# Stacked keys and queries written to neighbouring partitions in 4 KB runs

## The chip, the cores and the metric

The kernel runs on 1 core of one Trainium2 chip. The metric is the device time of one execution in microseconds (us). A change of about 1% is what a measurement of this kernel can tell from none.

## The reference

A gated cross-attention block and a feed-forward block, float32, over 64 sequences of 128 tokens with 256 features; 16 heads of 16. The causal mask is inside the attention, and the result of each block is added through a tanh gate:

```python
def _L0_xattn_ref(q, k, v, Wq, Wk, Wv, Wo, bo):
    qh = jnp.einsum('bse,hed->bhsd', q, Wq)
    kh = jnp.einsum('bse,hed->bhsd', k, Wk)
    vh = jnp.einsum('bse,hed->bhsd', v, Wv)
    scores = jnp.einsum('bhsd,bhtd->bhst', qh, kh) / jnp.sqrt(d)
    scores = jnp.where(causal, scores, -1000000000.0)
    att = jax.nn.softmax(scores, axis=-1)
    out = jnp.einsum('bhst,bhtd->bhsd', att, vh)
    return concat(out) @ Wo.T + bo

def _L0_ffn_ref(x, ...):                       # _tlin(x, w, s) = einsum('bsi,oi->bso', x, w) * s
    h = silu(_tlin(x, w1_w, w1_s)) * _tlin(x, w2_w, w2_s)      # 256 -> 1024
    h = gelu(_tlin(h, h1_w, h1_s))                             # 1024 -> 1024
    h = gelu(_tlin(h, h2_w, h2_s))                             # 1024 -> 1024
    return _tlin(h, w3_w, w3_s)                                # 1024 -> 256

x = x + tanh(g_xattn) * _L0_xattn_ref(_layernorm(x), ctx, ctx, ...)
x = x + tanh(g_ffn) * _L0_ffn_ref(_layernorm(x), ...)
```

## The kernel before

Two sequences ("rows", `ROWS = 2`) make a block, and there are 32 blocks. While the feed-forward of block n - 1 runs, the attention of block n is computed, and its projections for block n + 1 are begun. All engines walk through one list written by hand, `ORDER` (`PROLOGUE` for the first block): each engine picks out the steps that are its own and runs them in that order. A "+" behind a step means that it works for the next block. The waits between the engines are semaphores.

The steps that matter here are these. `Q` and `K` project queries and keys on TensorE (PE). ScalarE writes their high part in a rounded float32, and VectorE the rest, the low part, to `q_parts` and `k_parts`, which hold [128 features, part, row, half of the features, 128 tokens]. To score at nearly full float32 precision, a head needs high and low parts of queries against high and low parts of keys, four products, and the kernel stacks them in the contraction dimension: `q4` and `k4` hold each feature four times, on different partitions (`COPIES = 4`), queries as high, low, high, low and keys as high, high, low, low. `k4` has, besides, an index e for the two halves of the features; entries of the other half are zero and stay so, from a memset at the start. In this way one matmul of 128 by 256 computes two heads.

[...]

- `write_parts` (steps `qw` and `kw`) waits until the parts are ready and until the copies of the block before have landed, and writes 512 KB to `q_saved` or `k_saved` (L338).
- `place_parts` (steps `kr.0`, `qr.0`, `qr.1`, `kr.1`: keys or queries of row 0 or 1) waits for this write and for the scores that still read the old copies, and issues the transfers back: for keys, 8 a row of 64 KB (L356), for queries, 4 a row of 128 KB (L351), all in runs of 1 KB. Copy number c fills the partitions c, c + 4, c + 8 and so on.
- In `scores` (steps `S.0` to `S.7`, L939), PE waits, at the first step of each row (S.0 and S.4), for all copies of queries and keys of that row; 16 counts a transfer.

In ORDER the issues of SP come as `D.6 ... D.7 kr.0+ qr.0+ qr.1+ lr+` at the end of one walk and `kr.1 lc+ lx+ D.0 lt+` at the start of the next. `D.t` is the transpose of the probabilities of step t by DMA (L366), and waits for POOL's parts of them and for PE's products with the values (`PV`, L955); `lr` loads the residual xres (L324), `lc`, `lx` and `lt` load the inputs of the next block. PE meets S.0 just ahead of the last feed-forward layer (`L4`) of the same walk, and S.4 between the third and the fourth output tile of the first one (`L1`). `rx` is POOL's addition to xres (L453).

Of the kernel before, what the change touches and what calls it, by code (L numbers as in the profile page):

```python
# [11 lines left out]
F32 = mybir.dt.float32  # L12
F32R = mybir.dt.float32r
# [5 lines left out]
P = 128  # L19
ROWS = 2  # L20
# [39 lines left out]
def program(nc, x, xT_in, cT_in, gains, attn_w, bo, w_all, scale_cols, w3s, out):  # L60
# [5 lines left out]
    KE = E // P  # L66
    KF = F // P
    NQ = ROWS * H // 4
    QROW = H // 4
# [16 lines left out]
    HALF = P // 2  # L86
# [3 lines left out]
    with ExitStack() as ctx:  # L90
        def sb(name, shape, dt=F32):
            return ctx.enter_context(nc.sbuf_tensor(name, shape, dt))
# [4 lines left out]
        def sem(name):  # L97
            return ctx.enter_context(nc.semaphore(name))
# [32 lines left out]
        COPIES = 4  # L131
        q_parts = sb("q_parts", [P, 2, ROWS, KE, P], F32R)
        k_parts = sb("k_parts", [P, 2, ROWS, KE, P], F32R)
        q4 = sb("q4", [P, ROWS, QROW, KE, P], F32R)
        k4 = sb("k4", [P, ROWS, QROW, 2, KE, P], F32R)
        q_saved = nc.dram_tensor("q_saved", [P, 2, ROWS, KE * P], F32, kind="Internal").ap()
        k_saved = nc.dram_tensor("k_saved", [P, 2, ROWS, KE * P], F32, kind="Internal").ap()
        vs = sb("vs", [P, ROWS, H, VCOLS], BF16)
        v_rest = sb("v_rest", [P, ROWS, E])
        PSLOTS = 4  # L140
# [68 lines left out]
        q_placed = [sem("q_placed0"), sem("q_placed1")]  # L209
        k_placed = [sem("k_placed0"), sem("k_placed1")]  # L210
# [35 lines left out]
        def wait(eng, s, value):  # L246

            if not isinstance(value, int) or value > 0:
                eng.wait_ge(s, value)
# [55 lines left out]
        def _(sp):  # L305
            def hold(s, value):
                if not isinstance(value, int) or value > 0:
                    sp.wait_ge(s, value)
                    sp.sem_inc(sp_waited)  # L309
# [21 lines left out]
            def write_parts(n, kind):  # L331

                parts, saved = (q_parts, q_saved) if kind == "qw" else (k_parts, k_saved)
                hold(*((q_hi_ready, KE * n + KE) if kind == "qw" else (k_hi_ready, n + 1)))
                hold(*((q_lo_ready, KE * n + KE) if kind == "qw" else (k_lo_ready, n + 1)))
                for placed in q_placed if kind == "qw" else k_placed:
                    hold(placed, 16 * COPIES * (1 if kind == "qw" else 2) * n)
                sp.dma_start(saved.rearrange("p a r x -> p (a r x)"),  # L338
                             parts[:].rearrange("p a r m t -> p (a r m t)").bitcast(F32))\
                    .then_inc(q_written if kind == "qw" else k_written, 16)  # L340

            def place_parts(n, kind, row):

                if kind == "kr" and isinstance(n, int) and n == 0 and row == 0:
                    sp.wait_ge(keys_cleared, 1)
                hold(q_written if kind == "qr" else k_written, 16 * n + 16)
                for ready in scores_ready:
                    hold(ready, NQ // 2 * n + QROW // 2 * (row - 1))
                for copy in range(COPIES):
                    if kind == "qr":  # L350
                        sp.dma_start(q4[copy:P:COPIES, row].rearrange("p j m t -> p j (m t)").bitcast(F32),  # L351
                                     q_saved[:, copy % 2, row].rearrange("(p j) x -> p j x", j=QROW))\
                            .then_inc(q_placed[row], 16)
                    else:
                        for e in range(2):
                            sp.dma_start(k4[e * HALF + copy:(e + 1) * HALF:COPIES, row, :, e]  # L356
                                         .rearrange("p j m t -> p j (m t)").bitcast(F32),
                                         k_saved[e * HALF:(e + 1) * HALF, copy // 2, row]
                                         .rearrange("(p j) x -> p j x", j=QROW)).then_inc(k_placed[row], 16)

            def transpose_probs(n, t):

# [17 lines left out]
            def body(n, ffn_on=True, attn=True, next_head=True, weights=False):  # L380
                for kind, k, ahead in table(n):
                    blk = n + ahead
                    here = next_head if ahead else attn
                    if kind == "lx" and here and not (isinstance(blk, int) and blk == 0):
                        load_x(blk)
                    if kind == "lt" and here and not (isinstance(blk, int) and blk == 0):
                        load_xT(blk)
                    if kind == "lr" and here:
                        load_residual(blk)
                    if kind == "lc" and here and not (isinstance(blk, int) and blk == 0):  # L390
                        load_c(blk)
                    if kind in ("qw", "kw") and here:
                        write_parts(blk, kind)
                    if kind in ("qr", "kr") and here:
                        place_parts(blk, kind, k)
                    if kind == "D" and here:
                        transpose_probs(blk, k)
                    if kind == "mv" and ffn_on:
                        move_x1(n - 1)
                    if kind == "sy" and not (isinstance(n, int) and n < 2):  # L400
                        store(n - 2)
# [8 lines left out]
            with sp.If(sp.value_load(flag[0:1, 0:1]) > 0):  # L410
                sp.wait_ge(chunk_rounded, CHUNKS)
                sp.wait_ge(chunk_tested, CHUNKS)
                for i in range(CHUNKS, 2 * CHUNKS):
                    slot, use = i % STAGES, i // STAGES
                    at = i % CHUNKS * CHUNK
# [484 lines left out]
        def _(pe):  # L900
# [30 lines left out]
            def scores(n, t):  # L931

                row, j = t // QROW, t % QROW
                wait(pe, masked_ready, n * NQ + t - 1)
                if j == 0:
                    wait(pe, q_placed[row], 16 * COPIES * (n + 1))
                    wait(pe, k_placed[row], 16 * COPIES * 2 * (n + 1))
                for m in range(KE):
                    last = pe.matmul(s_bank[t % SBANKS][:, m * TOK:(m + 1) * TOK].rearrange("p (e t) -> p e t", e=2),  # L939
                                     q4[:, row, j, m], k4[:, row, j, :, m], start=True, stop=True)  # L940
                last.then_inc(scores_ready[t % SBANKS], 1)

            def probs_values(n, t):
# [15 lines left out]
            def run(general, first):  # L959
# [17 lines left out]
                def body(n, ffn_on=True, attn=True, next_head=True, weights=False):  # L977
# [8 lines left out]
                    for kind, k, ahead in table(n):  # L986
# [38 lines left out]
                        if kind == "S" and here:  # L1025
                            scores(blk, k)
# [89 lines left out]
```

## Time and profile before

| | |
|---|---|
| Median of 3 runs | 1858.6 us (1854.09 to 1867.01) |
| The profiled execution | 1868.9 us, its span 1867.1 us |
| Busy share: PE, VectorE, ScalarE, GpSimd | 93%, 74%, 71%, 58% |
| Mean granted TensorE clock | 0.975 |
| Transfers of keys a block | 16 of 64 KB |
| Transfers of queries a block | 8 of 128 KB |
| Write of each to DRAM a block | 1 of 512 KB |

How to read it: one execution was recorded by the hardware profiler. Times are us from the start of the span. PE is TensorE's matmuls, PEld its weight loads, DVE VectorE, ACT ScalarE, POOL GpSimd, SP SyncE, and "SPq" SyncE's queue of instructions, which holds the DMA issues. L939 is line 939 of the kernel. A block is 54.8 us from 200 us on. The "chain" is followed back from the last instruction, at each step to what released it.

### The profile page before, as it was taken

How to read it: one execution, taken by the hardware profiler on the slowest of the kernel's cores; microseconds unless marked ns; L12 is line 12 of the kernel's file. 1: busy time of each engine (PE TensorE's matmuls, PEld its weight loads, DVE VectorE, ACT ScalarE, POOL GpSimd, SP SyncE). 2: the span in 40 equal slices, each digit the busy share in tenths (PEclk: the TensorE clock that was granted, in tenths of full speed). 3: DMA queues.
4: the chain of work that ended last, by engine and by line, in shares of the span. 5: the costliest groups of instructions: out<-in, count | busy, mean ns of one | idle time of the engine just before them, and what ended most of it. 6: DMA issues, size and time to landing. Idle time of an engine off the chain costs nothing.

```text
span 1867.1 us, 39954 instructions
## 1 busy us (share of the span) xinstructions
PE 1730.6 (93%) x11014; PEld 1482.3 (79%) x11014; DVE 1389.0 (74%) x3059; ACT 1319.2 (71%) x3014; POOL 1075.4 (58%) x1389
## 2 busy tenths in 40 slices
PE   3279999999999999999999999999999999999998
PEld 2268888888888888888888888888888888888876
DVE  4477777788777777877777877777777777787774
ACT  3356777777677877777777767777767777776764
POOL 2365556655555666555665655566555566565552
PEclk7579999999999999999999999999999999999999
DMA  8944544445444444454444545444445444454420
GB/s 281 152 125 114 142 114 115 125 118 139 125 125 120 119 113 135 124 140 115 117 124 115 140 118 138 116 115 125 118 124 140 115 119 125 112 140 118 125 53 16
DMA packets 399643, 231.39 MB, mean 124 GB/s; under 512 B 287232, under 2 KB 377600, under 8 KB 398080
## 3 DMA queue, kind: packets, MB, share of 16 engines
q1 hardware_dynamic: 397456, 219.25, 45.6%
q10 hardware_dynamic: 2160, 11.81, 2.2%
q8 instruction: 13, 0.21, 0.1%
q14 instruction: 14, 0.11, 0.0%
HBM read 113.53 MB, written 41.94 MB: 83 GB/s over the span
## 4 chain that ended last, share of the span: by engine, by line
PE 56%; SPq 29%; issue 6%; DMA 6%; DVE 1%; POOL 1%; ACT 0%; POOLq 0%; DVEq 0%
PE ffn L964 45%; SPq L356 15%; SPq L351 8%; PE work L904 6%; SPq L366 4%; DMA k<-k_saved 4%; DMA pT<-p_parts 2%; PE s_bank L939 2%; PE pv L955 2%; SPq L324 1%; SPq L309 0%; PE work L1044 0%; DMA aw<-in_attn_w 0%; DVE full L639 0%; DVE full L632 0%
## 5 line engine op out<-in xcount | busy, mean ns | idle before, releaser
L964 PE MATMUL ffn<-hb,W 128*128 128x512 f32 x2048 | 510.5, 399 | 1.2 <-POOL hb L501 1.2
L964 PE MATMUL ffn<-ha,W 128*128 128x512 f32 x2048 | 477.9, 393 | 1.3 <-POOL ha L496 1.3
L964 PEld LDWEIGHTS ffn<-ha,W 128*128 128x128 f32 x2048 | 382.0, 188 | 84.4 <-POOL ha L496 2.7
L646 DVE TENSOR_REDUCE full<-ffn 128x256 f32<-128x512 f32 x512 | 346.2, 686 | 136.7 <-PE ffn L964 107.3
L964 PEld LDWEIGHTS ffn<-hb,W 128*128 128x128 f32 x2048 | 375.6, 188 | 77.0 <-POOL hb L501 2.1
L809 ACT ACTIVATE probs<-probs,exp_bias 128x128 f32<-128x128 f32 x1024 | 323.8, 391 | 81.9 <-DVE exp_bias L614 80.7
L464 POOL TENSOR_TENSOR p_parts<-probs,p_parts 128x512 f16<-128x512 f32 x256 | 301.6, 1178 | 20.4
L462 POOL CAST p_parts<-probs 128x512 f16<-128x512 f32 x256 | 157.2, 614 | 207.4 <-ACT probs L809 165.0
L604 DVE SCALAR_TENSOR_TENSOR probs<-s_bank,rstd,causal 128x512 f32<-128x512 f32 x256 | 191.4, 748 | 97.4 <-PE s_bank L939 96.9
L964 PE MATMUL ffn<-x2T_hi,W 128*128 128x256 f32 x1024 | 253.3, 286 | 0.7 <-DVE x2T_lo L742 0.5
L827 ACT ACTIVATE full<-full,cols 128x256 f32<-128x256 f32 x512 | 253.4, 495 | 0.0
L964 PE MATMUL ffn<-x2T_lo,W 128*128 128x256 f32 x1024 | 251.4, 283 | 0.0
L501 POOL TENSOR_TENSOR hb<-full,hb 128x256 fp32r<-128x256 f32 x256 | 189.2, 739 | 84.1 <-ACT full L827 75.3
L496 POOL TENSOR_TENSOR ha<-full,ha 128x256 fp32r<-128x256 f32 x256 | 185.8, 740 | 38.0 <-ACT ha L841 34.1
L826 ACT ACTIVATE ha<-full,cols 128x256 fp32r<-128x256 f32 x256 | 129.3, 505 | 107.0 <-DVE full L646 106.6
L964 PEld LDWEIGHTS ffn<-x2T_hi,W 128*128 128x128 f32 x1024 | 195.9, 191 | 2.7 <-DVE y L714 0.8
L964 PEld LDWEIGHTS ffn<-x2T_lo,W 128*128 128x128 f32 x1024 | 196.0, 191 | 0.0
L612 DVE TENSOR_REDUCE negmax<-probs 128x4 f32<-128x512 f32 x256 | 173.8, 679 | 2.2
L939 PE MATMUL s_bank<-k,q 128*128 128x256 f32 x512 | 113.9, 315 | 64.5 <-DMA k<-k_saved 39.7
L850 ACT ACTIVATE full<-ffn,half_s 128x256 f32<-128x256 f32 x256 | 119.5, 467 | 47.0 <-PE ffn L964 46.0
L964 PE MATMUL ffn<-W,ha 128*128 128x256 f32 x1024 | 146.7, 288 | 6.1 <-DVE full L646 6.0
L826 ACT ACTIVATE hb<-full,cols 128x256 fp32r<-128x256 f32 x256 | 128.2, 501 | 31.7 <-DVE full L646 30.7
(81 smaller groups left out, 2413.2 us busy)
## 6 DMA issues: line engine op xcount, KB each, us to landing
k<-k_saved SPq DMA_DIRECT2D x512, 64.0 KB, 2.3
q<-q_saved SPq DMA_DIRECT2D x256, 128.0 KB, 2.7
k_saved<-k_parts SPq DMA_DIRECT2D x32, 512.0 KB, 2.7
q_saved<-q_parts SPq DMA_DIRECT2D x32, 512.0 KB, 2.7
wnat<-in_ffn_w ACTq DMA_DIRECT2D x11, 1024.0 KB, 11.7
xT<-in_x_T SPq DMA_DIRECT2D x32, 256.0 KB, 3.2
cT<-in_ctx_T SPq DMA_DIRECT2D x32, 256.0 KB, 2.7
x_in<-in_x SPq DMA_DIRECT2D x32, 256.0 KB, 2.9
```

Of the source, the lines that this page charges most:

```text
L356: sp.dma_start(k4[e * HALF + copy:(e + 1) * HALF:COPIES, row, :, e] .rearrange("p j m t -> p j (m t)").bitcast(F32), k_saved[e * HALF:(e + ...
L462: pool.tensor_copy(p_parts[:, t % 2, 0], probs[:, t % PSLOTS]).then_inc(p_hi_ready, 1)
L464: pool.tensor_tensor(p_parts[:, t % 2, 1], probs[:, t % PSLOTS], p_parts[:, t % 2, 0], ALU.subtract)\
L496: pool.tensor_tensor(ha_lo[:, k], full[:, k % 4], ha_hi[:, k], ALU.subtract)\
L501: pool.tensor_tensor(hb_lo[:, k], full[:, k % 4], hb_hi[:, k], ALU.subtract)\
L604: dve.scalar_tensor_tensor(probs[:, slot], s_bank[t % SBANKS][:].rearrange("p (h t) -> p h t", h=4), rstd[:, t // QROW:t // QROW + 1], cau ...
L612: dve.tensor_reduce(negmax[:, slot], probs[:, slot], AX_X, ALU.max, negate=True).then_inc(max_ready, 1)
L646: dve.tensor_reduce(full[:, m % 4], src[:].rearrange("p (a t) -> p t a", a=2), AX_X, ALU.add).then_inc(done, 1)
L809: last = act.activation(probs[:, slot, h], probs[:, slot, h], ACT.Exp, bias=exp_bias[:, slot, h:h + 1])
L826: act.activation(hi[:, m], f, ACT.Gelu, scale=scales[:, m:m + 1]).then_inc(hi_sem, 1)
L827: act.activation(f, f, ACT.Gelu, scale=scales[:, m:m + 1]).then_inc(hi_sem, 1)
L964: return pe.matmul(dst, w, h, **flags)
```

## The change

Three edits. The tensors in DRAM are laid out [part, row, feature, ...] and not [feature, part, row, ...]. The four copies of a feature no longer lie on four neighbouring partitions: each half of 64 partitions has its groups of 16 partitions by copy, and partition d of a group holds the four features 4d to 4d + 3 in its four slots j, which lie one behind the other in DRAM (4 KB). So one transfer fills 32 neighbouring partitions, for queries with the high and then the low part, for keys with the same part twice (a repeat with a step of zero in the source). And in `k4` the index e stands ahead of j, so that the 4 KB are in one piece there too. Keys take 4 transfers of 128 KB a row and not 8 of 64 KB; queries stay at 4 of 128 KB. The number in the wait for the keys follows. ORDER is the same.

```diff
-        k4 = sb("k4", [P, ROWS, QROW, 2, KE, P], F32R)
-        q_saved = nc.dram_tensor("q_saved", [P, 2, ROWS, KE * P], F32, kind="Internal").ap()
-        k_saved = nc.dram_tensor("k_saved", [P, 2, ROWS, KE * P], F32, kind="Internal").ap()
+        k4 = sb("k4", [P, ROWS, 2, QROW, KE, P], F32R)
+        q_saved = nc.dram_tensor("q_saved", [2, ROWS, P, KE * P], F32, kind="Internal").ap()
+        k_saved = nc.dram_tensor("k_saved", [2, ROWS, P, KE * P], F32, kind="Internal").ap()
...
                 for placed in q_placed if kind == "qw" else k_placed:
-                    hold(placed, 16 * COPIES * (1 if kind == "qw" else 2) * n)
-                sp.dma_start(saved.rearrange("p a r x -> p (a r x)"),
-                             parts[:].rearrange("p a r m t -> p (a r m t)").bitcast(F32))\
+                    hold(placed, 16 * COPIES * n)
+                sp.dma_start(saved.rearrange("a r p x -> p (a r) x"),
+                             parts[:].rearrange("p a r m t -> p (a r) (m t)").bitcast(F32))\
                     .then_inc(q_written if kind == "qw" else k_written, 16)
...
-                for copy in range(COPIES):
-                    if kind == "qr":
-                        sp.dma_start(q4[copy:P:COPIES, row].rearrange("p j m t -> p j (m t)").bitcast(F32),
-                                     q_saved[:, copy % 2, row].rearrange("(p j) x -> p j x", j=QROW))\
-                            .then_inc(q_placed[row], 16)
-                    else:
-                        for e in range(2):
-                            sp.dma_start(k4[e * HALF + copy:(e + 1) * HALF:COPIES, row, :, e]
-                                         .rearrange("p j m t -> p j (m t)").bitcast(F32),
-                                         k_saved[e * HALF:(e + 1) * HALF, copy // 2, row]
-                                         .rearrange("(p j) x -> p j x", j=QROW)).then_inc(k_placed[row], 16)
+                for e in range(2):
+                    for copy in range(2):
+                        at = e * HALF + copy * HALF // 2
+                        if kind == "qr":
+                            src = q_saved[:, row, e * HALF:(e + 1) * HALF].rearrange("a (d j) x -> a d (j x)", j=QROW)
+                            sp.dma_start(q4[at:at + HALF // 2, row].rearrange("p j m t -> p (j m t)").bitcast(F32), src)\
+                                .then_inc(q_placed[row], 16)
+                        else:
+                            src = k_saved[copy, row, e * HALF:(e + 1) * HALF].rearrange("(d j) x -> d (j x)", j=QROW)
+                            sp.dma_start(k4[at:at + HALF // 2, row, e].rearrange("p j m t -> p (j m t)").bitcast(F32),
+                                         src.unsqueeze(0).broadcast_to([2, HALF // QROW, QROW * KE * P]))\
+                                .then_inc(k_placed[row], 16)
...
-                    wait(pe, k_placed[row], 16 * COPIES * 2 * (n + 1))
+                    wait(pe, k_placed[row], 16 * COPIES * (n + 1))
...
-                                     q4[:, row, j, m], k4[:, row, j, :, m], start=True, stop=True)
+                                     q4[:, row, j, m], k4[:, row, :, j, m], start=True, stop=True)
```

## Rows read from the trace of the kernel before

**Rows 1.** The page: span, TensorE, the chain's shares, and POOL's longest group.

```profile
span 1867.1 us, 39954 instructions
...
PE 1730.6 (93%) x11014; PEld 1482.3 (79%) x11014; DVE 1389.0 (74%) x3059; ACT 1319.2 (71%) x3014; POOL 1075.4 (58%) x1389
...
PE 56%; SPq 29%; issue 6%; DMA 6%; DVE 1%; POOL 1%; ACT 0%; POOLq 0%; DVEq 0%
...
L464 POOL TENSOR_TENSOR p_parts<-probs,p_parts 128x512 f16<-128x512 f32 x256 | 301.6, 1178 | 20.4
```

**Rows 2.** The chain that ended last, one block: start us, us, what.

```profile
978.38 1.23 SPq L366
...
996.52 2.18 DMA k<-k_saved
...
998.75 0.51 PE s_bank L939 x2
```

**Rows 3.** PE's timeline: start us, us, instructions, idle before in brackets.

```profile
990.13 0.50 PE L939 MATMUL s_bank<-k,q 128*128 128x256 f32 x2 [0.20 <-DMA q<-q_saved]
...
998.75 0.51 PE L939 MATMUL s_bank<-k,q 128*128 128x256 f32 x2 [1.23 <-DMA k<-k_saved]
```

**Rows 4.** Waits of PE, 1200 to 1748.4 us: us in total, times, longest.

```profile
PE s_bank L939 <- DMA k<-k_saved: 13.3, 10, 1.9
PE s_bank L939 <- DMA q<-q_saved: 2.3, 10, 0.4
```

**Rows 5.** Stretches: us, busy us by engine, granted clock, DMA share, GB/s.

```profile
974.40:1029.20 54.80, 53.19 (x346) 45.78 (x345) 42.34 (x96) 40.72 (x95) 33.16 (x44) 1.00 0.47 124
...
976.00:977.00 1.00, 1.00 (x21) 0.90 (x20) 0.00 (x0) 0.88 (x4) 0.92 (x2) 1.00 1.06 417
...
992.00:999.00 7.00, 5.77 (x49) 5.55 (x48) 6.70 (x16) 5.96 (x16) 4.71 (x6) 1.00 0.47 136
...
20.00:30.00 10.00, 0.44 (x2) 0.44 (x3) 5.48 (x3) 1.91 (x1) 0.00 (x0) 0.67 0.89 274
...
110.50:115.60 5.10, 5.10 (x24) 5.10 (x25) 3.59 (x7) 3.44 (x11) 3.02 (x3) 0.50 0.32 103
115.80:121.70 5.90, 5.30 (x45) 5.13 (x44) 4.22 (x10) 3.79 (x9) 5.07 (x7) 1.00 1.05 211
```

**Rows 6.** Timeline of SyncE's queue over the same block: start us, us, issues.

```profile
974.40 0.41 SPq L378 DMA_DIRECT2D out<-y  x1
975.29 0.33 SPq L338 DMA_DIRECT2D q_saved<-q_parts  x1
976.80 2.80 SPq L366 DMA_TRANSPOSE pT<-p_parts  x2
980.05 5.02 SPq L356 DMA_DIRECT2D k<-k_saved  x8
985.42 5.19 SPq L351 DMA_DIRECT2D q<-q_saved  x8
990.78 0.46 SPq L324 DMA_DIRECT2D xres<-in_x  x1
992.09 5.03 SPq L356 DMA_DIRECT2D k<-k_saved  x8
```

**Rows 7.** The page's DMA issues: KB each, median us from issue to landing.

```profile
k<-k_saved SPq DMA_DIRECT2D x512, 64.0 KB, 2.3
q<-q_saved SPq DMA_DIRECT2D x256, 128.0 KB, 2.7
k_saved<-k_parts SPq DMA_DIRECT2D x32, 512.0 KB, 2.7
q_saved<-q_parts SPq DMA_DIRECT2D x32, 512.0 KB, 2.7
```

**Rows 8.** Waits of the whole span, POOL's for the residual.

```profile
POOL xres L453 <- DMA xres<-in_x: 97.1, 30, 4.5
```

**Rows 9.** Block 0: timelines of SyncE's queue and of PE.

```profile
19.06 5.13 SPq L356 DMA_DIRECT2D k<-k_saved  x8
...
29.56 1.22 PE L939 MATMUL s_bank<-k,q 128*128 128x256 f32 x4 [10.93 <-DMA q<-q_saved]
...
43.29 0.89 PE L939 MATMUL s_bank<-k,q 128*128 128x256 f32 x2
```

## The prediction, made before the changed kernel ran

> **What bounds the kernel now.** I read the page first, then the chain of work that ended last over one steady block, then the timelines of TensorE and of SyncE's queue over the same block, then the waits, the landings of the transfers and, last, stretches for the load of the DMA engines. The page [rows 1] gives PE 93% of the span, and the chain 56% PE and 29% SyncE's queue. So PE is the bound and is nearly full, but the thread that fixes its pace runs through the queue that issues the transfers. The chain [rows 2] shows the loop: PE ends a product with the values, the queue issues the transpose of the last probabilities at 978.38, and only then, in program order, the copies of keys and queries; the last copy of keys lands 2.18 us after its issue and frees the matmul of S.4 at 998.75. The PE timeline [rows 3] shows the price on PE: 0.20 us idle before S.0 (waiting for queries) and 1.23 us before S.4 (waiting for keys of row 1). Over ten blocks the waits [rows 4] are 13.3 us for keys and 2.3 us for queries, so 1.56 us a block. That is all that an earlier arrival can return; PE's other work fills the rest of a block of 54.80 us [rows 5].
>
> The queue's timeline [rows 6] has its work from 980.05 on: 8 keys issues (5.02 us), 8 queries issues (5.19 us, both rows), xres, 8 keys issues (5.03 us). One issue is (5.02 - 0.04) / 8, some 0.63 us with its gap. The DMA engines are busy for 0.47 of a block on average [rows 5]: they are no bound as long as each transfer is spread over all 16.
>
> **The change part by part.**
>
> *Fewer issues.* Eight of 16 keys issues go: 8 x 0.63 = 5.0 us of SyncE's queue a block, 2.5 us of it ahead of the queries and 2.5 us in the last group. If all else is equal, this takes the 1.56 us of waits away. Queries stay at eight issues. Bytes stay: 512 KB of keys a row and block, in 4 transfers of 128 KB instead of 8 of 64 KB, and 4 x 128 KB of queries.
>
> *The spread over engines, the step that decides.* Read the shapes and not the sizes. Before, each copy has 16 partitions (keys) or 32 partitions (queries) as its outer count on both sides: 16 engines can each be given an equal part. After, the destination is 32 neighbouring partitions, but the source is (2, 16, 1024): for queries the 2 are the high and the low parts, 256 KB apart, and for keys the 2 are a repeat with step zero. Neither folds with the 16 behind it. If the split is made along the outer count, a transfer has two parts, and so two engines, each with 16 runs of 4 KB. Should it always be the same two, they carry every byte of the keys and queries, one transfer behind the other. No transfer of the trace before has so small an outer count (the ones touched lead with 16, 32 or 128), so no row shows this; I take it as the likeliest for its shape alone: whatever deals out the parts by the outer count can't make 16 of 2.
>
> The Trainium skill speaks against this change in the same direction (DMA: Bandwidth & Descriptors, section Why a DMA increments its semaphore by 16 and not by 1, and the row "Use all 16 engines" of its Rules for kernel authors): the engine count is the largest up to 16 that divides the slowest count of both sides, the lowest-numbered engines are used, and a leading zero-stride broadcast of c copies confines a DMA to c engines. By that rule k is 2 here, always the same pair; no row of before shows a case of it.
>
> *Price of a confined transfer.* The nearest rows for long runs are of 976 to 977 us, where the store of the output and the 512 KB write of q_saved, in 4 KB runs, stand back to back on the same queue: 417 GB/s at a share of 1.06 [rows 5]. That is 417 / 16 = 26.1 GB/s for one engine, with no gap between two transfers. 128 KB is 131,072 bytes; half of it is 65,536 bytes, / 26.1 = 2.51 us. The other end is the rate with 1 KB runs: 992 to 999 us moved 136 GB/s at a share of 0.47, so 136 / 0.47 / 16 = 18.1 GB/s, which makes 3.62 us. The runs are 4 KB, so I take 2.51. A block has 16 such transfers: 40.2 us on two engines.
>
> *What is late, and by how much.* From the first keys issue (980.05) to S.4 (998.75) are 18.7 us now. After: 0.6 us for the first issue; about 0.3 us of the transposes still under way (0 to 1); 16 x 2.51 = 40.2; xres, which stands among them (256 KB over 16 engines at 18.1 GB/s is 0.9); and 2.1 us of latency, the 2.3 us to landing of a 64 KB copy [rows 7] less the 0.23 us that its 4 KB an engine takes. Sum 44.1 us, so S.4 starts 25.4 us later. Half way, S.0 needs the first eight: 0.6 + 0.3 + 20.1 + 2.1 = 23.1, at 1003.2 instead of 990.13, 13.0 us later; this is inside the 25.4 and not on top of it. PE is in order: behind S.0 stand the last layer (L4), X2, S.1 to S.3 and the first L1 steps, 998.75 - 1.23 - 990.13 = 7.4 us, which fit between the two waits. Behind S.4 stands everything to the next keys issue, 54.8 - 18.7 = 36.1 us that shift with PE. POOL waits for xres (97.1 us in 30 times now [rows 8]); it lands near 1014. Behind it are four POOL operations; even at 1178 ns each, that of the split [rows 1], they end before 1020, so S.4 stays the last. cT, x_in and the first transposes queue up behind the keys; some 3 us of engine time that K and PV don't need before 5 to 7 us after S.4.
>
> *The clock.* In the first block PE sat idle for 10.93 us ahead of S.0 [rows 9]; in 20 to 30 us the granted clock is 0.67 (a fall from 2.4 to 1.2 GHz on the way), and 0.50 in 110.5 to 115.6, where 24 matmuls take 5.10 us; at full clock 45 take 5.30 us [rows 5], so 24 take 2.8. Two idle stretches of that kind in every block would take the clock down each time. After S.0 the 7.4 us at half speed are under 15 us and still end at about 1018, ahead of 1024; after S.4 up to 5.10 - 2.8 = 2.3 us are lost. I take 1.5 (0 to 2.3).
>
> *Small parts.* The write of q_saved and k_saved now goes out in 1 KB runs: 32 KB an engine at 18.1 instead of 26.1 GB/s, 1.8 instead of 1.25 us. Its landing (2.7 us, [rows 7]) has cover: issued at 975.29, read from 982 on at the earliest. Without cover it would be 0.55 us. The matmul reads the keys in two runs of 128 with another step, 282 ns or so before and after: nothing. The wait counts change by number only. SyncE's 5.0 us are gained and hidden behind the landing.
>
> *Sum.* 25.4 + 1.5 = 26.9 us a block. Copies for blocks 1 to 31 are made in steady order: 31 x 26.9 = 834. Block 0 has its copies in the prologue: first keys issue 19.06, S.4 at 43.29 [rows 9]; with 44.1 us it is at 63.2, 20 us later, and the weight loads share the engines (274 GB/s at 0.89 in 20 to 30 us); I take 25 (0 to 50). The profiled execution took 1868.9 us with a span of 1867.1: 1868.9 + 834 + 25 = 2728. It is 10.3 us above the median of the three runs, 1858.6, so the prediction is 2718, say **2720**.
>
> A check of the order: the two engines would be busy for 40.2 us, plus the rest of the block's traffic. Of 0.47 x 54.8 = 25.8 us, the keys and queries are now 2 MB / 16 / 18.1 GB/s = 7.2; 18.6 remain. 58.8 us is over the 54.8 of a block, so even with all waits hidden it could not be as fast as before: at least 4 x 31 = 124 us more, 1983.
>
> **The rivals.**
>
> *All 16 engines, as the text of the change has it.* Something splits the 32 partitions and not the 2, or the pair moves on from transfer to transfer. The last of queries row 0 is then issued 2.5 us earlier, S.0 waits for nothing; the last of keys row 1 is issued at about 992.0 and with 2.7 us lands at 994.7, ahead of 997.5 where PE gets there. It gains 1.56 x 31 = 48 us: 1810. For it: it is all that is needed, and a 128 KB copy of queries lands in 2.7 us now [rows 7]. Against it: the leading 2 of the source. It decides where S.4's wait is gone. It would be faster, the other side. Chance 0.11.
>
> *Only the keys confined* (the step of zero treated apart, queries on 16). The engine time up to S.4 is 8 x 2.51 + 8 x 0.45 + 0.9 = 24.6, with 3.0 around it 27.6: 8.9 us a block later, 276 in all, 2135. Against it: the two sources have the same counts. Chance 0.04.
>
> *Spread over 16, and nothing gained:* S.4 then waits for something else, such as slower writes into 32 neighbouring partitions; at 3 us more landing the 1.56 us would be gone. 1859. Chance 0.03.
>
> **How the numbers follow.** Confined to one pair has 0.82, and 2720 is its time. Its bounds: without clock loss and prologue 1859 + 31 x 25.4 = 2646; with some of the wait absorbed, or a rate a little above, down to 2450; with the 18.1 GB/s the transfers take 57.9 us and the time is 2720 + 31 x 17.7 = 3269, which I count only in part, as the runs are 4 KB: 3100. The range 2450 to 3100 leaves out the other three cases (0.18) and little of this one. About 1% is what a measurement of this kernel can tell from no change. Faster by over 1% is the first rival, 0.11; within 1% the third, 0.03; slower 0.82 + 0.04 = 0.86.
>
> **What the profile after would show.** To landing of a keys or queries copy 4.6 us where nothing is queued, and over 10 us in the median, as they queue up; PE idle about 13 us before S.0 and 6 to 13 us before S.4 (less when the clock is low between them), named by keys and queries; a block of about 82 us; PE under 70% busy; granted clock under 1.0 in every block; the mean share of the DMA engines lower, not higher; the keys issues 256. Wrong it is if the copies land in under 4 us and the block is near 53 us, which is the first rival; if queries land in 3 us and only keys late, it is the second.

## The result, and the profile after

The changed kernel takes 2755.2 us in the median of 4 runs (2750.0 to 2757.7), the kernel before on the same chips 1861.2 us. The ratio is 1.480, its 95% interval 1.474 to 1.486. The prediction was 2720 us, and the mechanism put first in it is the one that the profile shows.

The spans of the two profiled executions differ by 881 us (the medians by 894). Where they come from can be read from the first keys issue of each block. Before, that of block 1 is at 97.6 us and that of block 31 at 1750.9: 55.1 us a block. After, they are at 116.0 and 2604.9: 83.0 us a block. So 18.3 us are lost in block 0, 30 x 27.9 = 836 in the steady blocks, and 26.9 in block 31 and what follows it; together 881.

The page of the changed kernel, against [rows 1] and [rows 7]: span, busy shares, granted clock, the chain, and the issues of keys and queries.

```profile
span 2748.1 us, 39669 instructions
...
PE 1838.9 (67%) x11014; PEld 1594.0 (58%) x11014; DVE 1398.3 (51%) x3059; ACT 1316.8 (48%) x3014; POOL 1071.8 (39%) x1389
...
PEclk6587888988888988888888788878888887898889
...
PE 40%; SPq 34%; DMA 21%; issue 4%; DVE 1%; POOL 0%; ACT 0%; POOLq 0%; DVEq 0%
...
k<-k_saved SPq DMA_DIRECT2D x256, 128.0 KB
q<-q_saved SPq DMA_DIRECT2D x256, 128.0 KB
k_saved<-k_parts SPq DMA_DIRECT2D x32, 512.0 KB, 3.0
```

PE is busy for 108 us more, since part of its work runs at a lower clock, but it fills only two thirds of the span, and DMA's share of the chain has gone from 6% to 21%. For keys and queries the page has no time to landing any more; in the two experiments below that confine only one kind, the column is empty for that kind alone.

PE's timeline in one steady block, against [rows 3]: start us, us, idle before in brackets. The first is S.0, the second S.4.

```profile
1382.84 0.80 PE L940 MATMUL s_bank<-k,q 128*128 128x256 f32 x2 [13.77 <-DMA q<-q_saved]
...
1404.29 0.77 PE L940 MATMUL s_bank<-k,q 128*128 128x256 f32 x2 [12.36 <-DMA k<-k_saved]
```

Where PE waited for 0.20 and 1.23 us, it waits for 13.8 and 12.4.

SyncE's queue in the same block, against [rows 6]:

```profile
1359.20 2.72 SPq L358 DMA_DIRECT2D k<-k_saved  x4
1362.18 14.09 SPq L354 DMA_DIRECT2D q<-q_saved  x8
1376.46 2.15 SPq L324 DMA_DIRECT2D xres<-in_x  x1
1379.32 10.44 SPq L358 DMA_DIRECT2D k<-k_saved  x4
...
1441.69 2.60 SPq L358 DMA_DIRECT2D k<-k_saved  x4
```

The first four issues are as quick as those before (0.65 us each). Then the queue blocks: 8 queries issues take 14.09 us and not 5.19. The chain of the same block shows the step from free to blocked (start us, us, what): the third queries issue takes 0.92 us, and the fourth 2.29, which is about the time that one transfer needs. It has the landing of the last keys transfer too: 16.73 us after its issue, where it was 2.18 [rows 2].

```profile
1363.47 0.92 SPq L354
...
1364.42 2.29 SPq L354
...
1387.42 16.73 DMA k<-k_saved
```

Stretches of the same block, against [rows 5] (granted clock, DMA share and GB/s are the last three columns):

```profile
1359.20:1441.70 82.50, 56.19 (x346) 48.80 (x345) 42.55 (x97) 40.67 (x94) 33.08 (x44) 0.86 0.36 83
1364.00:1366.00 2.00, 2.00 (x12) 1.66 (x11) 1.53 (x4) 1.12 (x3) 0.10 (x1) 1.00 0.13 53
1366.00:1368.00 2.00, 1.82 (x9) 1.25 (x8) 1.61 (x4) 0.90 (x3) 1.15 (x1) 1.00 0.13 53
1370.00:1374.00 4.00, 0.00 (x0) 0.00 (x0) 0.00 (x0) 0.00 (x0) 0.00 (x0) 0.87 0.13 51
```

This is the line to look for. While the queue is full of keys and queries, the mean busy share of the 16 DMA engines is 0.13, that is 2 of 16 (0.125), and they move 51 to 53 GB/s, 26 a busy engine. The profile has no row for each engine, but this is what fourteen engines standing still and two at work would give. Several transfers were waiting all that time; were they on different pairs, the share would be higher, so it is one pair for all. In the kernel before, the share was 0.47 with the keys of row 1 on the queue [rows 5].

### The profile page after: what moved, and what is told of

Read it like the earlier page. It is cut to its first block, busy times and chain, and to the rows that moved or that the text cites. A ratio compares the mean times of both kernels' runs of the same rounds, so it can differ in the third digit from the quotient of the medians.

```text
span 2748.1 us, 39669 instructions
## 1 busy us (share of the span) xinstructions
PE 1838.9 (67%) x11014; PEld 1594.0 (58%) x11014; DVE 1398.3 (51%) x3059; ACT 1316.8 (48%) x3014; POOL 1071.8 (39%) x1389
## 4 chain that ended last, share of the span: by engine, by line
PE 40%; SPq 34%; DMA 21%; issue 4%; DVE 1%; POOL 0%; ACT 0%; POOLq 0%; DVEq 0%
PE ffn L965 33%; DMA k<-k_saved 19%; SPq L354 16%; SPq L358 12%; PE work L905 4%; SPq L367 3%; SPq L324 2%; PE s_bank L940 2%; PE pv L956 1%; DMA cT<-in_ctx_T 1%; DMA pT<-p_parts 1%; SPq L309 0%; PE work L1045 0%; DMA aw<-in_attn_w 0%; POOL p_parts L465 0%
## 5 line engine op out<-in xcount | busy, mean ns | idle before, releaser
L940 PE MATMUL s_bank<-k,q 128*128 128x256 f32 x512 | 130.6, 352 | 834.1 <-DMA q<-q_saved 452.9
L940 PEld LDWEIGHTS s_bank<-k,q 128*128 128x128 f32 x512 | 94.4, 223 | 851.5 <-DMA q<-q_saved 427.3
L454 POOL TENSOR_TENSOR xres<-xres,bo_tg 128x512 f32<-128x512 f32 x32 | 42.5, 1327 | 728.4 <-DMA xres<-in_x 728.4
L633 DVE SCALAR_TENSOR_TENSOR full<-full,ffn 128x256 f32<-128x256 f32 x256 | 107.2, 419 | 430.5 <-ACT full L851 423.9
L878 ACT ACTIVATE x2T_hi<-work 128x256 fp32r<-128x256 f32 x64 | 24.6, 384 | 576.6 <-PE work L1045 576.6
L965 PE MATMUL ffn<-x2T_hi,W 128*128 128x256 f32 x1024 | 298.2, 320 | 0.5 <-DVE x2T_lo L743 0.5
L965 PE MATMUL ffn<-x2T_lo,W 128*128 128x256 f32 x1024 | 293.9, 315 | 0.0
L965 PEld LDWEIGHTS ffn<-x2T_hi,W 128*128 128x128 f32 x1024 | 234.9, 229 | 1.6 <-DVE x2T_lo L743 0.7
L965 PEld LDWEIGHTS ffn<-x2T_lo,W 128*128 128x128 f32 x1024 | 232.8, 227 | 0.0
```

Source lines behind the costliest of these rows:

```text
L965: return pe.matmul(dst, w, h, **flags)
```

## The experiments

Each was timed beside the kernel before, on the same chip.

**Exchange the two outer dimensions.** Nothing else changes: the same bytes, run length, number of transfers and set of 32 partitions; on them the two parts now lie interleaved.

```diff
-src = q_saved[:, row, e * HALF:(e + 1) * HALF].rearrange("a (d j) x -> a d (j x)", j=QROW)
+src = q_saved[:, row, e * HALF:(e + 1) * HALF].rearrange("a (d j) x -> d a (j x)", j=QROW)
...
-             src.unsqueeze(0).broadcast_to([2, HALF // QROW, QROW * KE * P])
+             src.unsqueeze(1).broadcast_to([HALF // QROW, 2, QROW * KE * P])
```

> The changed kernel with the two outer dimensions of each source exchanged (16 feature groups outside, the 2 inside); the two parts lie interleaved on the 32 partitions. Bytes, runs of 4 KB, number of transfers (4 a row for keys and for queries), partitions as a set and the writes to DRAM stay. Theory 'outer count sets the number of engines': transfers are back on 16 engines, waits of PE for keys and queries vanish, near 1810 us (1795 to 1830), block near 53.3 us, issues of 0.6 us. Rival 'neighbouring partitions': writing into 32 neighbours is what is slow, it stays near 2755. Rival 'a repeated source is slow': keys stay slow, queries recover, near 2110.

Measured: 1813.1 us, ratio 0.974 (0.968 to 0.980). The page and SyncE's queue of this kernel:

```profile
k<-k_saved SPq DMA_DIRECT2D x256, 128.0 KB, 2.8
q<-q_saved SPq DMA_DIRECT2D x256, 128.0 KB, 2.7
...
PE 83%; DVE 8%; issue 4%; DMA 2%; POOL 1%; ACT 1%; DVEq 0%; SPq 0%; POOLq 0%; ACTq 0%
```

```profile
1211.58 2.50 SPq L358 DMA_DIRECT2D k<-k_saved  x4
1214.34 5.14 SPq L354 DMA_DIRECT2D q<-q_saved  x8
1220.84 0.41 SPq L324 DMA_DIRECT2D xres<-in_x  x1
1221.96 2.46 SPq L358 DMA_DIRECT2D k<-k_saved  x4
...
1265.58 2.50 SPq L358 DMA_DIRECT2D k<-k_saved  x4
```

PE's waits of this kernel over ten blocks, 1200 to 1740 us, against [rows 4]:

```profile
PE ffn L965 <- DVE x2T_lo L743: 2.9, 10, 0.4
PE ffn L965 <- DVE full L647: 1.8, 10, 0.2
PE ffn L965 <- DVE y L715: 1.3, 6, 0.3
```

The whole loss is gone, and both waits for keys and queries with it; the queue's share of the chain falls from 29% before to 0%. The block is 54.0 us. Rivals that blame the neighbouring partitions or the repeat in the source fall: both are still there. Timed again beside other runs it was the same:

> e1_outer16 unchanged, to see its gain once more beside the others, probably on another chip: ratio to the kernel before 0.974 again, near 1813 us.

Measured: 1812.0 us, ratio 0.974 (0.969 to 0.980).

**The same partitions, transfers cut in their halves.** To be sure that the interleaving doesn't matter, each transfer of the changed kernel is issued as two of 16 partitions, which leaves every byte where the change puts it (counts in the waits doubled).

```diff
+for a in range(2):
+    src = q_saved[a, row, e * HALF:(e + 1) * HALF].rearrange("(d j) x -> d (j x)", j=QROW)
+    sp.dma_start(q4[at + a * 16:at + a * 16 + 16, row]..., src)     # keys likewise
```

> The changed kernel with exactly the same bytes on the same partitions, but each transfer of 32 partitions cut in its two halves of 16 (outer count 16 on both sides, 64 KB): 16 transfers of keys and 16 of queries a block. Outer count theory: all on 16 engines, the loss is gone. By the 0.44 us issues seen for such transfers in e2_queries_outer2 the last keys issue of a block ends some 15.7 us after the first, landing at 17.8 against 18.7 before: 1820 to 1840. Rival 'the arrangement on neighbouring partitions is slow': stays far above 1861. Rival 'the number of issues sets the time': with 32 issues in place of 24, slower than before, 1900.

Measured: 1843.3 us in the median of ten runs from 1828.8 to 1853.4, ratio 0.992 (0.989 to 0.994), 3 us over the expected stretch. Its queue:

```profile
1223.93 3.57 SPq L360 DMA_DIRECT2D k<-k_saved  x8
1227.76 7.36 SPq L355 DMA_DIRECT2D q<-q_saved  x16
...
1236.54 3.55 SPq L360 DMA_DIRECT2D k<-k_saved  x8
```

The loss is gone here too, so the place on the partitions costs nothing. 32 issues are a little faster than 24 before (0.8%, which is less than the 1% that one measurement tells from none): a transfer to 16 neighbouring partitions takes 3.57 / 8 = 0.45 us to issue, one with two outer dimensions some 0.63. What goes with the time is not the count of issues, but when the last one is out: 16.2 us after the first keys issue here, 17.1 before, and 12.8 in the first experiment.

**Only one kind confined.** First queries with the 2 outside and keys in halves of 16 partitions, then the other way round. The edits to the changed kernel, the first for keys, the second for queries:

```diff
-sp.dma_start(k4[at:at + HALF // 2, row, e]..., src.unsqueeze(0).broadcast_to([2, HALF // QROW, QROW * KE * P]))
+for a in range(2):
+    sp.dma_start(k4[at + a * 16:at + a * 16 + 16, row, e]..., src)
```

```diff
-sp.dma_start(q4[at:at + HALF // 2, row]..., src)
+for a in range(2):
+    src = q_saved[a, row, e * HALF:(e + 1) * HALF].rearrange("(d j) x -> d (j x)", j=QROW)
+    sp.dma_start(q4[at + a * 16:at + a * 16 + 16, row]..., src)
```

> The changed kernel with keys in 8 transfers a row of 16 partitions each (outer count 16 on both sides, no repeat in the source, 4 KB runs); queries stay with the 2 outside. Outer count theory: 8 transfers a block are confined to one pair of engines, and queue there: S.4 comes 0.6 + 4.8 + 8 x 2.51 + 0.9 + 1.3 + 2.1 = 29.8 us after the first keys issue and not 18.7, so 11 us a block, 1861 + 31 x 11 = 2200, up to 2270 with the clock's fall. Rival 'a repeated source is slow': near 1861. Rival 'neighbouring partitions': queries are still 32 neighbours, keys 16 neighbours, near 2755.

Measured: 2344.0 us, ratio 1.259 (1.250 to 1.269).

> The changed kernel with queries in 8 transfers a row of 16 partitions each (outer count 16 on both sides, 4 KB runs); keys stay with the repeat of 2 outside. Outer count theory: S.4 comes 26.6 us after the first keys issue and not 18.7, so 8 us a block, 1861 + 31 x 8 = 2109, up to 2170 with the clock's fall and the prologue. Were each kind on a pair of engines of its own, this and e2_queries_outer2 would each keep about half of the loss of the change or more, 2300 or above; with one pair for both, the two losses together are less than the whole, since part of each wait is hidden. Rival 'a repeated source is slow': nearly all the loss stays, near 2700.

Measured: 2283.0 us, ratio 1.227 (1.217 to 1.236).

Each kind is confined by itself, with the repeat in the source and without it; so the step of zero is not the point. But both are 75 to 175 us above what was expected of them, 2 to 6 us a block, and their sum, 483 + 422 = 905 us over the kernel before, is not less than the whole loss (894). The time is in the transfers: in the second kernel S.4 comes 30.4 us after the first keys issue, and not 26.6. The first keys issue, S.4 and stretches of that kernel:

```profile
1264.64 2.60 SPq L359 DMA_DIRECT2D k<-k_saved  x4
...
1295.00 0.58 PE L941 MATMUL s_bank<-k,q 128*128 128x256 f32 x2 [2.05 <-DMA k<-k_saved]
```

```profile
1271.00:1273.00 2.00, 2.00 (x10) 1.45 (x8) 1.76 (x3) 0.99 (x3) 0.73 (x1) 1.00 0.56 166
1275.00:1277.00 2.00, 0.00 (x0) 0.00 (x0) 0.00 (x0) 0.00 (x0) 0.22 (x1) 1.00 0.56 161
1286.00:1292.00 6.00, 6.00 (x43) 5.97 (x42) 4.94 (x11) 4.14 (x10) 1.63 (x3) 0.80 0.13 52
```

While spread transfers run beside the confined ones, a busy engine moves 166 / 0.56 / 16 = 18.5 GB/s, and when the pair is alone, 52 / 0.13 / 16 = 25. My estimate used 26 throughout. The 18.5 is a mean over all busy engines and does not show the pair's own rate. That the pair too was slower is an estimate: from 1267 to 1294 us the share in stretches of 1 us is never under 0.12, so the pair was never idle, and up to S.4 each of its engines has 8 x 64 KB of keys, 16 x 4 KB of queries and 16 KB of xres to move, 606,000 bytes in 27 to 28 us, some 22 GB/s. That covers the sign and about the size of the miss; what the engines contend for (the DRAM side, or the gaps between short shares) no run here tells apart.

The sum of the two losses was to be less than the whole with one pair for both. In the mean of blocks 5 to 29 of the traces it is, as far as the transfers go: S.4 comes 31.9 and 30.7 us after the first keys issue instead of 18.8, which is 13.1 + 11.9 = 25.0 us later against 26.0 in the changed kernel (44.8 us). But behind S.4 each of the three kernels loses 1.4 to 2.0 us a block besides (38.2, 37.6 and 38.0 us instead of 36.2 to the next keys issue), and so the sum has this loss twice. That keys and queries did not have a pair each is shown by the changed kernel itself: its share stays at 0.13 from 1364 us on, when both kinds were waiting.

**Length of the runs against the number of issues.** The first experiment with keys in 8 transfers a row again, so 24 issues a block as before, but runs of 4 KB on 16 engines:

```diff
+for a in range(2):
+    sp.dma_start(k4[at + a:at + HALF // 2:2, row, e]..., src)
```

> e1_outer16 with keys in 8 transfers a row of 64 KB (16 partitions at a step of 2, outer count 16, 4 KB runs), so as many issues as before. It tells the number of issues from the length of the runs. Theory 'the wait is for the queue's issues': as before, within 1% of 1861, PE waits 1.2 to 1.6 us at S.4 for keys. Rival 'run length': long runs land so much earlier that it is as fast as e1_outer16.

Measured: 1852.2 us in the median of nine runs, ratio 0.994 (0.990 to 0.998). PE's waits over ten blocks, 1200 to 1740 us, of the profiled execution, which was the slowest of the nine (1867.2 us):

```profile
PE s_bank L940 <- DMA k<-k_saved: 11.7, 10, 1.4
...
PE s_bank L940 <- DMA q<-q_saved: 0.6, 3, 0.3
```

Of the 1.56 us of waits a block [rows 4], 1.2 are still there. Runs of 4 KB bring 0.3 us a block at most (9 us in all, less than the 1% that one measurement tells from none), the eight issues fewer the rest. That is the part of the change which was sound.

**The clock's part.** PE idles twice a block in the changed kernel, and the clock falls. To take this alone, matmuls that nobody reads were put in ahead of the two waits, in time that PE has to spare there.

```diff
+if j == 0 and not (isinstance(n, int) and n == 0):
+    for i in range(40):                        # second try: 60 if row == 0 else 53
+        pe.matmul(s_bank[t % SBANKS][:], W[:, 0:P], W[:, 0:BANK], start=True, stop=True)
```

> The changed kernel as it is, as the base for e6_filled on the same chip: near 2755 us.

Measured: 2761.5 us, ratio 1.485 (1.480 to 1.490).

> The changed kernel with 40 matmuls of 512 columns put in ahead of PE's wait at S.0 and at S.4 (their results are overwritten); at full clock they take some 8.6 us, less than the 13.8 and 12.4 us for which PE waits there anyway. It measures the clock's part alone. Theory 'the fall of the clock costs 1.3 to 1.5 us a block, after S.4': the granted clock goes from 0.83 to near 0.95 or more, and 31 x 1.4 = 43 us come back, near 2712. Rival 'the block's end is set by the transfers, the clock costs nothing': within 1% of e7_change_again with 10 us or less gained.

Measured: 2752.3 us, ratio 1.479 (1.473 to 1.486), only 9 us less. This run doesn't decide: up to 4.6 and 3.3 us of idle time were left ahead of S.0 and S.4, and the clock was still at half right behind S.4. PE's timeline there shows matmuls at 0.41 us:

```profile
1411.11 0.77 PE L943 MATMUL s_bank<-k,q 128*128 128x256 f32 x2 [3.25 <-DMA k<-k_saved]
1411.67 0.41 PE L968 MATMUL ffn<-x2T_hi,W 128*128 128x256 f32 x1
```

So the idle time had to be filled further:

> e6_filled left 4.6 us of PE idle ahead of S.0 and 3.3 us ahead of S.4, and the clock was still at half behind S.4 (matmuls of the next layer at 410 ns). Here 60 matmuls stand ahead of S.0 (13 us at full clock) and 53 ahead of S.4 (11.5 us), so that less than 1 us of either wait is left idle. Theory 'the clock's fall costs 1.3 to 2.8 us a block after S.4': the matmuls behind S.4 run at 280 ns, from S.4 to the next keys issue it is 36.1 us again as before the change, and the time is 40 to 85 us under the changed kernel on the same chip. Rival 'the clock costs nothing': within 10 us of it.

> The changed kernel as it is, as the base for e9_filled_more on the same chip: near 2760 us.

Measured: 2704.2 us filled (ratio 1.455, 1.447 to 1.464) against 2758.2 us (ratio 1.482, 1.473 to 1.491) as it is. Stretches of 800 us, first the changed kernel, then the filled one:

```profile
1200.00:2000.00 800.00, 541.87 (x3266) 473.11 (x3265) 406.53 (x904) 383.66 (x890) 313.28 (x407) 0.83 0.36 81
```

```profile
1200.00:2000.00 800.00, 781.36 (x4533) 661.26 (x4531) 422.50 (x946) 407.06 (x939) 331.85 (x429) 1.00 0.37 85
```

With the clock at 1.00 throughout (2.4 GHz), the time falls by 54 us, 54 / 31 = 1.7 us a block. The other 26 us a block are the transfers. S.4 and the next keys issue of the filled kernel show where the 1.7 us were:

```profile
1389.61 0.48 PE L943 MATMUL s_bank<-k,q 128*128 128x256 f32 x2 [1.74 <-DMA k<-k_saved]
...
1425.74 2.59 SPq L358 DMA_DIRECT2D k<-k_saved  x4
```

Between them are 36.1 us, as in the kernel before; in the changed kernel it is 38.0 us in the mean of blocks 5 to 29.

## Why the prediction was right, point by point

*The spread.* The deciding step, two outer parts and so two engines, held: share 0.13, and two lines that exchange the outer dimensions take the loss away. The Trainium skill's rule (DMA: Bandwidth & Descriptors, Why a DMA increments its semaphore by 16 and not by 1: the largest count up to 16 that divides both sides' slowest dimension) agrees with every kernel here: a share of 0.13 with an outer 2 on one side, and landings of 2.2 to 2.8 us with 16 or 32 on each side. Its claim that these are the lowest-numbered engines can't be seen in the profile. That it is one and the same pair follows from the share of 0.13 while several transfers wait.

*The price of a confined transfer.* Predicted 2.51 us by 26.1 GB/s an engine. The stretches give 53 / 2 = 26.5 GB/s, 2.47 us. The nearness is in part luck: the 417 GB/s stood at a share of 1.06, and I did not divide by it as I did for the 18.1; with it the rate is 24.6 GB/s and the time 2.66 us. Besides, those rows were writes to DRAM, and the copies are reads.

*What is late.* Predicted: S.0 23.1 us and S.4 44.1 us after the first keys issue. Measured: 1382.84 - 1359.20 = 23.6, and 1404.29 - 1359.20 = 45.1; in the mean of blocks 5 to 29 S.4 comes after 44.8 us (18.8 before).

*The clock.* Predicted 1.5 us a block (0 to 2.3), measured 1.7 by the filled kernel. I had PE's 7.4 us between the waits take up to 15; they take 21.45 - 12.36 = 9.1, since the clock comes back on the way; this is hidden in either case. From S.4 to the next keys issue it is 37.4 us in this block and 38.0 in the mean, instead of 36.1 and 36.2.

*The sum.* Predicted 25.4 + 1.5 = 26.9 us a block, measured 27.9, of which 26.0 come up to S.4. In all 859 us were predicted and 881 measured between the profiled executions. 2755 is 37 us above 2718: these 22, and 15 because the profiled execution before lay 10.3 us above the median of its runs and the one after 5.2 us below.

*Block 0* was predicted at 25 us and measured at 18.3, but that it is so near is luck. By the sum S.4 was to start 44.1 us after the first keys issue, at 63.2. It started 61.8 us after it, at 80.7 instead of 43.3, since PE stood 28.3 us for the first queries and 25.3 us for cT, which came behind the copies. In 80.7 to 116.0 us half of this was made up, for the kernel before needs 54.4 us there, in which PE waits for other things (10.2 us for POOL alone). PE's timelines, first of the changed kernel, then of the kernel before:

```profile
46.04 1.22 PE L940 MATMUL s_bank<-k,q 128*128 128x256 f32 x4 [28.25 <-DMA q<-q_saved]
...
77.53 3.75 PE L905 MATMUL work<-cT,aw 128*128 128x256 f32 x8 [25.27 <-DMA cT<-in_ctx_T]
80.72 0.99 PE L940 MATMUL s_bank<-k,q 128*128 128x256 f32 x2
```

```profile
58.67 0.49 PE L955 MATMUL pv<-vs,pT 128*128 128x49 bf16 x8 [10.23 <-POOL vs L485]
```

*SyncE's queue* is the step that failed. I gave it 5.0 us a block gained and hidden. In its place the queue lost time: issues of about 2.3 us each, the time of one transfer, from the eighth on, so 30.6 us for the 17 issues from the first keys to the last (1359.20 to 1389.76), against 17.1 us before for 25. In a steady block it cost nothing: in the filled kernel the queue is blocked alike, and from S.4 to the next keys issue it is 36.1 us as before. In block 0 cT was issued 19 us later than before (54.62 and not 35.49) and PE waited for it; how much of that is the blocked queue and how much the copies ahead of cT, no run tells apart.

*The signs.* PE idle before S.0 and S.4 (13.8 and 12.4 us), PE under 70% (67%), the clock (0.83), a block of about 82 us (83.0) and 256 keys issues came as forecast. Time to landing was to be above 4.6 us and over 10 in the median; the page gives none for these transfers. The one landing that the chain shows is 16.7 us, which agrees, and the empty place in the page's column was a sign that I had not listed.

*The writes* in 1 KB runs land after 3.0 us instead of 2.7, where I had 0.55 us more. The first experiment has them as well and is faster than the kernel before, so they are covered.

*The first rival* (all 16 engines, 1810 us) was priced right: the exchange of two dimensions measured 1813. *The second*, only the keys confined, was priced at 2135 and is 2283: its failing term is the pair's rate while spread transfers run beside it, 18.5 GB/s an engine and not 26.

*The bound by occupation* alone (58.8 us a block) was far below the result: what counted was not that two engines were full all the time, but that the chain waits for all sixteen transfers in a row and then for 36 to 38 us of other work.

## What to carry to other kernels

Write the outer dimension of a transfer on both sides as 16 or 32, the counts that were at full spread here (of smaller ones only 2 was run); a pair of parts or a repeat belongs inside it, not outside. With that, fewer and longer transfers won 2.6% here; without it the same transfers cost 48%, and nothing but the order of two dimensions lies between. In the profile, look for a DMA share of 0.13 with a full queue: low use of the DMA engines can be the sign of a transfer bound.

## What the runs showed of the hardware that was not expected

- The queue of issues holds only some transfers ahead: with 128 KB each on two engines, the seventh issue was slow (0.92 us) and the eighth to the twelfth took 2.1 to 2.4 us, about the time of one transfer. SyncE is then blocked for everything behind. Whether the limit counts transfers or their runs, no run tells.
- An issue's time goes by the shape: about 0.45 us for 16 neighbouring partitions with one run each, about 0.63 us with a second outer dimension (5.14 us for 8 in the first experiment) or a step of 2 between the partitions (4.96 us for 8 in the kernel with keys in 8 transfers a row).
- A busy DMA engine moves 25 to 26 GB/s in 4 KB runs when only two are at work, and 18.5 GB/s in the mean of all busy ones while spread and confined transfers run together, with the same runs. In the first experiment, with all transfers spread, it is 176 / 0.62 / 16 = 17.7 GB/s from 1212 to 1226 us.
- Filling idle time with spare matmuls gave back little until nearly all of it was filled: with 3 to 5 us of it left, the clock was still at half behind the wait, and 9 us came back; with under 2 us left, 54.
